# Attention products moved from VectorE to GpSimd, the token statistics of the next tile moved behind those of the last, and a finer final conversion

## The chip, the cores and the metric

One Trainium2 chip, all 8 cores. Each core takes 2,048 of the 16,384 tokens and runs the same program; no core talks to another. The metric is the device time of the slowest core in microseconds (us).

## The reference

```python
def _layernorm(x, axis=-1, eps=1e-5):
    m = jnp.mean(x, axis=axis, keepdims=True)
    v = jnp.var(x, axis=axis, keepdims=True)
    return (x - m) / jnp.sqrt(v + eps)

# attention: the 16 heads of ONE token attend to each other, D_K = 64
qkv = (jnp.einsum('bsd,de->bse', x, W_qkv) + b_qkv).reshape(B, S, 16, 3 * 64)
q, k, v = (qkv[..., :64], qkv[..., 64:128], qkv[..., 128:])
scores = jnp.einsum('bshd,bsgd->bshg', q, k) / np.sqrt(64)
attn = jax.nn.softmax(scores, axis=-1)
context = jnp.einsum('bshg,bsgd->bshd', attn, v).reshape(B, S, 1024)
attn_out = jnp.einsum('bsd,de->bse', context, W_out) + b_out

# ffn: 8 experts, all of them for every token, summed
h = jax.nn.silu(x @ wg) * (x @ wu);  acc = acc + h @ wd     # 1024 -> 4096 -> 1024

x = x + _layernorm(attn_ref(_layernorm(x)))
x = x + _layernorm(ffn_ref(_layernorm(x)))
```

The input is 16,384 tokens of 1,024 float32 numbers.

## The kernel before

The program is written as one list of instructions for each engine, with semaphores placed by hand. Each engine works through its list strictly in order, so the order of the calls in the source is the order on each engine. It has three stages.

Stage A is the attention, over 16 tiles of 128 tokens, tokens on the partitions. A tile t goes through: S1 (layer norm of the input, `ln_stats` at L141 and the write of `ln1` at L230), S2 (8 transposes on TensorE at L206 and their copy out of PSUM by VectorE at L209), S3 (54 matmuls for q, k and v, L253 and L257, each of 6 groups copied to `qkv` by ScalarE at L262), S4 (the attention proper, on VectorE), S5 (transposes of `ctxt`, the output projection at L359), S6 (layer norm of the projection and its addition to `xf`, L163 to L379) and S7 (the second layer norm, transposes into `ln2T`; for every fourth tile SyncE spills `xf` to HBM and loads new tokens).

S4 first copies v into `vtc` in another order (L272). Then, for 4 groups of 4 heads, it multiplies q by k into a 4,096-wide bf16 product `prod` (L283), halves it by three additions (L287) and sums the last 8 columns into `scores` (L292). `prod` has two slots, so group n may be written once group n-2 has been summed. A softmax follows (L297 to L311), its Exp on ScalarE (L305), and then 4 groups of the product with v (L325, L329, L337). In the kernel before all of this but the Exp is VectorE's.

The layer norms pass through ScalarE: L154 and L156 (Ln and Exp on a column) sit in ScalarE's list behind whatever stands before them. The loop at L406 sets that list:

```python
    S1(0)
    for t_i in range(nt_lim):
        S2(t_i)
        S3(t_i)
        if t_i + 1 < nt_lim:
            S1(t_i + 1)
        if t_i >= 1:
            S6(t_i - 1)
            S7(t_i - 1)
        S4(t_i)
        S5(t_i)
```

Stage B is the feed-forward part. 64 blocks of weights (8 experts by 8 slices of 512) are loaded by GpSimd's queue into double buffers; for each block and each of 4 groups of 512 tokens (jj), TensorE makes gate and up products (L498, L503), ScalarE the silu (L509), VectorE the product `hbuf` (L513), and TensorE the down product (L529), which VectorE adds to `acc` in SBUF (L539). The down product of a group runs one group behind.

Stage C waits until all of `acc` is written, converts it to bf16 on ScalarE in 8 rows of 2,048 (L583), and then takes 16 tiles: 8 transposes (L600), copy, layer norm on VectorE (L604 to L625), the addition of the spilled `xf` (`xrel`, loaded per tile at L593), and the store (L634).

Of the kernel before, what the change touches and what calls it, by code (L numbers as in the profile page):

```python
# [26 lines left out]

def build(mode='full', nt_lim=NT):
    nc = bass.Bass("TRN2", target_bir_lowering=False)
    x_d = nc.dram_tensor("x", [T, D], F32, kind="ExternalInput").ap()  # L30
    wqkv_d = nc.dram_tensor("wqkv", [D, H3], F32, kind="ExternalInput").ap()
    bqkv_d = nc.dram_tensor("bqkv", [H3], F32, kind="ExternalInput").ap()
    wout_d = nc.dram_tensor("wout", [D, D], F32, kind="ExternalInput").ap()
# [49 lines left out]
    XLa = Ch("XLa"); XLb = Ch("XLb")  # L83
    STa = Ch("STa"); STb = Ch("STb")
    STD = Ch("STD")
    XC = Ch("XC")
    SP = Ch("SP")
    STp = [None, None]
    WI = Ch("WI")
# [31 lines left out]
    ps_mm = Pa("ps_mm", [128, 2, 512], F32)  # L121
    ps_att = Pa("ps_att", [128, 2, 2, 512], F32)

    x_r = x_d.rearrange("(j i p) d -> p j i d", p=128, i=4)
    xsp_r = xsp_d.rearrange("(j i p) d -> p j i d", p=128, i=4)
    op('y', lambda e: e.dma_start(xf[:, 0], x_r[:, 0]), XLa, 16)
    op('y', lambda e: e.dma_start(xf[:, 1], x_r[:, 1]), XLb, 16)
    op('g', lambda g: g.dma_start(wqkv_sb[:], wqkv_d.rearrange("(k p) e -> p k e", p=128)), WI, 16)
# [139 lines left out]
    def S4(t_i):  # L268
        p2 = t_i % 2
        QE.wt('v', tok_qkv_ev_last[t_i])  # L270
        qb = 3072 * p2
        op('v', lambda v, qb=qb: v.tensor_copy(  # L272
            vtc[:].rearrange("p (d g) -> p d g", g=16),
            bass.AP(qh, qb + 128, [[2 * H3, 128], [1, 64], [192, 16]])), VV)
        for grp in range(4):
            h0 = grp * 4
            gg = n_hg[0]; n_hg[0] += 1
            sl = gg % 2
            if gg - 2 in tok_prod:
                VV.wt('v', tok_prod[gg - 2])  # L280
            qap = bass.AP(qh, qb + 192 * h0, [[2 * H3, 128], [192, 4], [0, 16], [1, 64]])
            kap = bass.AP(qh, qb + 64, [[2 * H3, 128], [0, 4], [192, 16], [1, 64]])
            op('v', lambda v, sl=sl, qap=qap, kap=kap: v.tensor_tensor(  # L283
                prod[:, sl].rearrange("p (h g d) -> p h g d", h=4, g=16), qap, kap, ALU.mult), VV)
            VV.wt('v')
            for half in (32, 16, 8):
                op('v', lambda v, sl=sl, half=half: v.tensor_add(  # L287
                    bass.AP(prod, sl * 4096, [[8192, 128], [1024, 4], [64, 16], [1, half]]),
                    bass.AP(prod, sl * 4096, [[8192, 128], [1024, 4], [64, 16], [1, half]]),
                    bass.AP(prod, sl * 4096 + half, [[8192, 128], [1024, 4], [64, 16], [1, half]])), VV)  # L290
                VV.wt('v')
# [22 lines left out]
        VV.wt('v')  # L314
        if t_i >= 2:
            TB.wt('v', tok_ctx_tr[t_i - 2])
        for grp in range(4):
            h0 = grp * 4
            gg = n_hg[0]; n_hg[0] += 1
            sl = gg % 2  # L320
            if gg - 2 in tok_prod:
                VV.wt('v', tok_prod[gg - 2])
            pap = bass.AP(ph, 16 * h0, [[256, 128], [16, 4], [0, 64], [1, 16]])
            vap = bass.AP(vtc, 0, [[1024, 128], [0, 4], [16, 64], [1, 16]])
            op('v', lambda v, sl=sl, pap=pap, vap=vap: v.tensor_tensor(  # L325
                prod[:, sl].rearrange("p (h d g) -> p h d g", h=4, d=64), pap, vap, ALU.mult), VV)
# [349 lines left out]
```

How the kernel before makes its waits and increments, by code:

```python
        def wt(self, k, tok=None):  # L71
            t_ = self.v if tok is None else tok
            em(k, lambda e, h=self.h, t=t_: e.wait_ge(h, t))
# [1 line left out]
    def op(k, fn, ch=None, n=1):  # L75
        if ch is not None:
            ch.v += n
            em(k, lambda e, fn=fn, h=ch.h, n=n: fn(e).then_inc(h, n))
            return ch.v
        em(k, fn)
        return None
```

## Time and profile before

| what | us |
|---|---|
| median of 3 runs | 7795.84 |
| lowest and highest run | 7694.49, 7986.77 |
| the profiled execution | 7065.31 |
| its span (slowest core, core 7) | 7063.7 |
| spans of the 8 cores | 7056.4 to 7063.7 |
| mean granted TensorE clock, every core | 0.905 |

The profiled execution is one run with its own record of every instruction. Its span runs from the first to the last instruction of the slowest core; 1.6 us of its time lie around the span. The eight cores agree, so one core may be read for all. The profiled execution is shorter than the lowest of the runs. Busy time of an engine is the sum of its instructions' durations; idle time is shown with the engine that released the wait.

### The profile page before, as it was taken

What the parts mean: (1) busy time and instruction counts of PE and PEld (TensorE: products, weight loads), DVE (VectorE), ACT (ScalarE), POOL (GpSimd) and SP (SyncE); (2) the same over time, 40 slices, a digit from 0 to 9 for tenths busy, and PEclk for the clock granted to TensorE, in tenths of its full rate; (3) what the DMA queues carried; (4) which work ended last, traced back from release to release, by engine and by line L of the source; (5) the groups of instructions that cost most, each with busy time, mean ns of one, the idle gap of its engine ahead of it and who ended that gap; (6) DMA issues with size and microseconds to landing.
All of it is one profiled execution on the core that took longest, in us unless ns stands there. A gap on an engine that the chain in (4) does not pass through costs nothing.

```text
span 7063.7 us, 71318 instructions; the slowest of 8 cores (7056.4 to 7063.7 us)
## 1 busy us (share of the span) xinstructions
PE 5675.5 (80%) x26240; PEld 2558.7 (36%) x26240; DVE 3241.3 (46%) x4484; ACT 745.9 (11%) x1291; POOL 165.0 (2%) x202
## 2 busy tenths in 40 slices
PE   2212222219999999999999999999999999999991
PEld 0000000104444444444444444444444444444441
DVE  3767666653343443434343434343434343443436
ACT  0000000001111111111111111111111111111111
POOL 0000000000000000000000000000000000000000
PEclk8556666659999999999999999999999999999995
DMA  3000000012223222222232222223322222232212
GB/s 71 0 24 0 24 0 12 0 25 41 36 39 46 42 36 36 36 36 36 42 47 38 36 36 36 36 36 45 46 36 36 36 37 36 39 46 42 36 19 95
DMA packets 178221, 247.85 MB, mean 35 GB/s; under 512 B 3808, under 2 KB 134880, under 8 KB 177888
## 3 DMA queue, kind: packets, MB, share of 16 engines
q0 software_dynamic: 169056, 209.74, 19.9%
q1 hardware_dynamic: 8832, 33.56, 1.4%
q8 instruction: 223, 3.65, 0.2%
q14 instruction: 110, 0.90, 0.0%
HBM read 436.22 MB, written 16.78 MB: 64 GB/s over the span
## 4 chain that ended last, share of the span: by engine, by line
PE 80%; DVE 14%; issue 3%; ACT 1%; another core or an unknown queue 1%; DMA 0%; DVEq 0%; ACTq 0%; POOL 0%; POOLq 0%
PE ps_g L498 25%; PE ps_u L503 25%; PE ps_d L529 25%; PE ps_mm L257 3%; DVE prod L329 2%; DVE prod L287 2%; DVE prod L325 2%; DVE prod L283 2%; PE ps_att L359 1%; PE ps_tr L206 1%; DMA wd_b<-wd 0%; PE ps_mm L253 0%; DVEq L73 0%; DVE tmpl L375 0%
## 5 line engine op out<-in xcount | busy, mean ns | idle before, releaser
L513 DVE TENSOR_TENSOR hbuf<-silb,ps_u 128x512 bf16<-128x512 bf16 x1024 | 704.7, 688 | 2886.4 <-PE ps_u L503 2845.8
L498 PE MATMUL ps_g<-ln2T,wg_b 128*128 128x512 bf16 x8192 | 1936.9, 379 | 35.8 <-DMA wd_b<-wd 35.8
L503 PE MATMUL ps_u<-ln2T,wu_b 128*128 128x512 bf16 x8192 | 1935.3, 379 | 0.0
L529 PE MATMUL ps_d<-hbuf,wd_b 128*128 128x512 bf16 x8192 | 1809.7, 379 | 0.0
L539 DVE TENSOR_TENSOR acc<-ps_d,acc 128x512 f32<-128x512 f32 x2016 | 1392.9, 692 | 330.6 <-PE ps_d L529 303.5
L498 PEld LDWEIGHTS ps_g<-ln2T,wg_b 128*128 128x128 bf16 x8192 | 801.7, 98 | 1003.4 <-issue 37.7
L503 PEld LDWEIGHTS ps_u<-ln2T,wu_b 128*128 128x128 bf16 x8192 | 801.8, 98 | 966.7 <-issue 0.7
L529 PEld LDWEIGHTS ps_d<-hbuf,wd_b 128*128 128x128 bf16 x8192 | 801.6, 98 | 966.5
L509 ACT ACTIVATE silb<-ps_g 128x512 bf16<-128x512 f32 x1024 | 611.3, 597 | 4675.2 <-PE ps_g L498 4675.2
L206 PE MATMUL ps_tr<-ident,ctxt 128*128 128x128 bf16 x128 | 16.2, 305 | 824.4 <-DVE ctxt L337 824.4
L206 PEld LDWEIGHTS ps_tr<-ident,ctxt 128*128 128x128 bf16 x128 | 12.3, 136 | 828.4 <-issue 828.4
L206 PE MATMUL ps_tr<-ident,ln2tok 128*128 128x128 bf16 x128 | 16.2, 305 | 274.9 <-DVE ln2tok L391 274.9
L470 POOL DMA_DIRECT2D wg_b<-wg x64 | 56.9, 890 | 6590.5 <-PE ps_d L529 5030.4
L257 PE MATMUL ps_mm<-wqkv_sb,ln1T 128*128 128x512 bf16 x768 | 184.2, 383 | 0.0
L329 DVE TENSOR_TENSOR prod<-prod 128x2048 bf16<-128x2048 bf16 (+2 forms) x192 | 162.3, 845 | 20.7 <-DVE prod L329 0.9
L287 DVE TENSOR_TENSOR prod<-prod 128x2048 bf16<-128x2048 bf16 (+2 forms) x192 | 149.9, 781 | 20.4 <-DVE prod L283 0.5
L325 DVE TENSOR_TENSOR prod<-probsn,vtc 128x4096 bf16<-128x4096 bf16 x64 | 146.3, 2286 | 3.7 <-DVE probsn L311 3.7
L283 DVE TENSOR_TENSOR prod<-qkv 128x4096 bf16<-128x4096 bf16 x64 | 146.1, 2282 | 0.0
L262 ACT ACTIVATE qkv<-ps_mm 128x512 bf16<-128x512 f32 x96 | 57.3, 597 | 695.0 <-PE ps_mm L257 695.0
L206 PEld LDWEIGHTS ps_tr<-ident,ln2tok 128*128 128x128 bf16 x128 | 12.4, 136 | 282.3 <-issue 282.3
L600 PE MATMUL ps_c<-ident,acc_bf 128*128 128x128 bf16 x128 | 16.0, 306 | 114.9 <-DVE acctok L604 99.2
L257 PEld LDWEIGHTS ps_mm<-wqkv_sb,ln1T 128*128 128x128 bf16 x768 | 67.6, 98 | 91.4 <-issue 24.2
(80 smaller groups left out, 974.2 us busy)
## 6 DMA issues: line engine op xcount, KB each, us to landing
wg_b<-wg POOLq DMA_DIRECT2D x64, 1024.0 KB, 12.4
wu_b<-wu POOLq DMA_DIRECT2D x64, 1024.0 KB, 18.2
wd_b<-wd POOLq DMA_DIRECT2D x64, 1024.0 KB, 22.2
xf<-x SPq DMA_DIRECT2D x4, 2048.0 KB, 13.9
xspill<-xf SPq DMA_DIRECT2D x4, 2048.0 KB, 6.9
xrel<-xspill SPq DMA_DIRECT2D x16, 512.0 KB, 3.9
out<-outb SPq DMA_DIRECT2D x16, 512.0 KB, 2.9
wqkv_sb<-wqkv POOLq DMA_DIRECT2D x1, 6144.0 KB, 53.5
```

Of the source, the lines that this page charges most:

```text
L206: tr_tok = op('t', lambda t, k=k, s_=s_: t.transpose(ps_tr[:, s_, k], src_fn(k), ident[:]), TB if k == 7 else None)
L257: mt = op('t', lambda t, n=n, b=b, k=k, p2=p2: t.matmul(ps_mm[:, b], ln1T[:, p2, k], wqkv_sb[:, k, n * 512:(n + 1) * 512], start=False, st ...
L283: op('v', lambda v, sl=sl, qap=qap, kap=kap: v.tensor_tensor(prod[:, sl].rearrange("p (h g d) -> p h g d", h=4, g=16), qap, kap, ALU.mult) ...
L287: op('v', lambda v, sl=sl, half=half: v.tensor_add(bass.AP(prod, sl * 4096, [[8192, 128], [1024, 4], [64, 16], [1, half]]), bass.AP(prod, ...
L325: op('v', lambda v, sl=sl, pap=pap, vap=vap: v.tensor_tensor(prod[:, sl].rearrange("p (h d g) -> p h d g", h=4, d=64), pap, vap, ALU.mult) ...
L329: op('v', lambda v, sl=sl, half=half: v.tensor_add(bass.AP(prod, sl * 4096, [[8192, 128], [1024, 4], [16, 64], [1, half]]), bass.AP(prod, ...
L498: gt = op('t', lambda t, par=par, kh=kh, kd=kd, bk=bk, toks=toks: t.matmul(ps_g[:, bk], wg_b[:, par, kd, kh * 128:(kh + 1) * 128], ln2T[:, ...
L503: ut = op('t', lambda t, par=par, kh=kh, kd=kd, bk=bk, toks=toks: t.matmul(ps_u[:, bk], wu_b[:, par, kd, kh * 128:(kh + 1) * 128], ln2T[:, ...
L509: silu_tok[c] = op('s', lambda s, bk=bk, c=c: s.activation(silb[:, c % 2], ps_g[:, bk], AF.Silu), SIL)
L513: mul_tok[c] = op('v', lambda v, kh=kh, bk=bk, c=c, q=q: v.tensor_tensor(hbuf[:, q % 2, kh], silb[:, c % 2], ps_u[:, bk], ALU.mult), MUL)
L529: dt_ = op('t', lambda t, par=par, m=m, mi=mi, kh=kh, q=q: t.matmul(ps_d[:, mi], wd_b[:, par, kh, m * 128:(m + 1) * 128], hbuf[:, q % 2, k ...
L539: tok = op('v', lambda v, m=m, mi=mi, toks=toks: v.tensor_add(acc[:, m, toks], ps_d[:, mi], acc[:, m, toks]), ACC)
```

## The change

Four things are edited. First, in S4 the copy into `vtc` and the four multiplications of q by k go from VectorE's list to GpSimd's, with a new semaphore GP; GpSimd waits for the last copy of q, k and v (QE), for the end of the previous tile's S4, and for `prod`'s slot. The three additions and the sum stay on VectorE. Second, S1 of the next tile is called after S6 and S7 of the last one. Third, in stage C the conversion is cut into 16 pieces of 8 by 128 columns, and each group of four pieces waits only for its own token group's last addition; `acc_bf` gets memory of its own from stage B's start, the transposes wait for their own piece, and `xrel` is loaded in 4 transfers of 2 MB with two slots, not 16 of 512 KB. Fourth, x, out and the spill lie in HBM as partition by tile by column.

```diff
-    x_d = nc.dram_tensor("x", [T, D], F32, kind="ExternalInput").ap()
+    x_d = nc.dram_tensor("x", [128, NT, D], F32, kind="ExternalInput").ap()
...
-    out_d = nc.dram_tensor("out", [T, D], F32, kind="ExternalOutput").ap()
-    xsp_d = nc.dram_tensor("xspill", [T, D], F32, kind="Internal").ap()
+    out_d = nc.dram_tensor("out", [128, NT, D], F32, kind="ExternalOutput").ap()
+    xsp_d = nc.dram_tensor("xspill", [128, NT, D], F32, kind="Internal").ap()
...
         QE.wt('v', tok_qkv_ev_last[t_i])
+        QE.wt('g', tok_qkv_ev_last[t_i])
+        if t_i >= 1:
+            VV.wt('g', tok_hm_done[t_i - 1])
         qb = 3072 * p2
-        op('v', lambda v, qb=qb: v.tensor_copy(
+        op('g', lambda g, qb=qb: g.tensor_copy(
             vtc[:].rearrange("p (d g) -> p d g", g=16),
-            bass.AP(qh, qb + 128, [[2 * H3, 128], [1, 64], [192, 16]])), VV)
+            bass.AP(qh, qb + 128, [[2 * H3, 128], [1, 64], [192, 16]])), GP)
...
             if gg - 2 in tok_prod:
-                VV.wt('v', tok_prod[gg - 2])
+                VV.wt('g', tok_prod[gg - 2])
...
-            op('v', lambda v, sl=sl, qap=qap, kap=kap: v.tensor_tensor(
-                prod[:, sl].rearrange("p (h g d) -> p h g d", h=4, g=16), qap, kap, ALU.mult), VV)
-            VV.wt('v')
+            op('g', lambda g, sl=sl, qap=qap, kap=kap: g.tensor_tensor(
+                prod[:, sl].rearrange("p (h g d) -> p h g d", h=4, g=16), qap, kap, ALU.mult), GP)
+            GP.wt('v')
...
-        if t_i + 1 < nt_lim:
-            S1(t_i + 1)
         if t_i >= 1:
             S6(t_i - 1)
             S7(t_i - 1)
+        if t_i + 1 < nt_lim:
+            S1(t_i + 1)
         S4(t_i)
...
-    ACC.wt('s', B_acc_done)
-    conv_tok = None
-    for mrow in range(8):
-        conv_tok = op('s', lambda s, mrow=mrow: s.activation(acc_bf[:, mrow], acc[:, mrow], AF.Copy),
-                      CS if mrow == 7 else None)
...
+    conv_tok = {}
+    for t_c in range(NT):
+        g_jj = t_c // 4
+        if t_c % 4 == 0:
+            ACC.wt('s', accw_tok[((NE * NG - 1) * NJ + g_jj, 1, 3)])
+        conv_tok[t_c] = op('s', lambda s, t_c=t_c: s.activation(
+            acc_bf[:, :, t_c * 128:(t_c + 1) * 128],
+            acc[:, :, t_c * 128:(t_c + 1) * 128], AF.Copy), CS)
...
+    for g_jj in range(2):
+        op('y', lambda e, g_jj=g_jj: e.dma_start(
+            xrel[:, g_jj % 2], xsp_r[:, g_jj]), XCa if g_jj % 2 == 0 else XCb, 16)
...
-        op('y', lambda e, t_i=t_i, p2=p2: e.dma_start(xrel[:, p2], xsp_t[:, t_i]), XC, 16)
         if t_i == 0:
-            CS.wt('t', conv_tok)
+            ACC.wt('t', B_acc_done)
+        CS.wt('t', conv_tok[t_i])
```

How the lists move. VectorE in stage A, around the head of a tile, before: `ln1T` is the copy that releases the q, k and v matmuls, `scr`/`stats` from `xf` are S1, `stats` from `ps_att` is S6.

```order
L209 COPY ln1T<-ps_tr 128x1024
L143 TENSOR_TENSOR scr<-xf 128x1024
L144 TENSOR_REDUCE stats<-xf 128x1
...
L158 TENSOR_SCALAR stats<-stats 128x1
L230 TENSOR_SCALAR ln<-xf,stats 128x1024
L163 TENSOR_REDUCE stats<-ps_att 128x1
L167 TENSOR_REDUCE stats<-scr 128x1
```

The same place of VectorE's list after the change (its line numbers are one higher there).

```order
L210 COPY ln1T<-ps_tr 128x1024
L164 TENSOR_REDUCE stats<-ps_att 128x1
L168 TENSOR_REDUCE stats<-scr 128x1
L169 TENSOR_SCALAR stats<-stats 128x1
L171 TENSOR_SCALAR stats<-stats 128x1
L172 TENSOR_TENSOR stats<-stats 128x1
L174 TENSOR_TENSOR stats<-stats 128x1
```

One reduction now stands between the copy and the next instruction that needs ScalarE (L168, which reads ScalarE's square); before, seven instructions of S1 stood between the copy and L158.

VectorE at the head of S4, before: the last copy of S7, then the copy of v, a product, its halvings and its sum.

```order
L209 COPY ln2T<-ps_tr 128x8x128
L272 COPY vtc<-qkv 128x1024
L283 TENSOR_TENSOR prod<-qkv 128x4096
L287 TENSOR_TENSOR prod<-prod 128x64x32
L287 TENSOR_TENSOR prod<-prod 128x64x16
L287 TENSOR_TENSOR prod<-prod 128x64x8
L292 TENSOR_REDUCE scores<-prod 128x64
```

The same place after: the end of S1, then the halvings at once, and GpSimd's own list for the same tile in the second piece.

```order
L159 TENSOR_SCALAR stats<-stats 128x1
L231 TENSOR_SCALAR ln<-xf,stats 128x1024
L291 TENSOR_TENSOR prod<-prod 128x64x32
L291 TENSOR_TENSOR prod<-prod 128x64x16
L291 TENSOR_TENSOR prod<-prod 128x64x8
L296 TENSOR_REDUCE scores<-prod 128x64
```

```order
L133 MEMSET ident 128x128
L135 AFFINE_SELECT ident<-ident 128x128
L276 COPY vtc<-qkv 128x1024
L287 TENSOR_TENSOR prod<-qkv 128x4096 x4
```

VectorE's five instructions of S4's head have become three kinds, and GpSimd, whose list held nothing between L135 and the weight loads, has a copy and four products per tile.

## Rows read from the trace of the kernel before

**Rows 1.** The page: busy time, share of the span and instructions by engine.
```profile
PE 5675.5 (80%) x26240; PEld 2558.7 (36%) x26240; DVE 3241.3 (46%) x4484; ACT 745.9 (11%) x1291; POOL 165.0 (2%) x202
```

**Rows 2.** Stretches of stages A, B and C; columns named in the first line.
```profile
core 7: us, PE busy (x) PEld busy (x) DVE busy (x) ACT busy (x) POOL busy (x), PEclk, DMA share, GB/s
0.00:1565.00 1565.00, 353.29 (x1536) 141.18 (x1536) 1011.91 (x1236) 108.09 (x225) 3.68 (x10) 0.63 0.06 15
1565.00:6906.00 5341.00, 5306.22 (x24576) 2405.08 (x24576) 2118.76 (x3071) 612.61 (x1025) 161.33 (x192) 1.00 0.26 39
6906.00:7064.00 158.00, 16.03 (x128) 12.46 (x128) 110.67 (x177) 25.20 (x41) 0.00 (x0) 0.53 0.30 106
```

**Rows 3.** Timeline of a tile: start, duration, engine, line; idle before in brackets.
```profile
529.59 0.69 DVE L209 COPY ln1T<-ps_tr 128x1024 bf16<-128x1024 bf16 x1 [8.36 <-PE ps_tr L206]
...
534.35 0.16 DVE L152 TENSOR_TENSOR stats<-stats 128x1 f32<-128x1 f32 x1
...
543.58 0.60 ACT L262 ACTIVATE qkv<-ps_mm 128x512 bf16<-128x512 f32 x1 [1.55 <-PE ps_mm L257]
...
544.86 0.21 DVE L158 TENSOR_SCALAR stats<-stats 128x1 f32<-128x1 f32 x1 [10.34 <-ACT stats L156]
...
547.28 1.02 ACT L165 ACTIVATE scr<-ps_att 128x1024 f32<-128x1024 f32 x1 [2.54 <-DVE stats L163]
...
550.12 0.16 DVE L173 TENSOR_TENSOR stats<-stats 128x1 f32<-128x1 f32 x1
...
554.26 1.23 DVE L143 TENSOR_TENSOR scr<-xf 128x1024 f32<-128x1024 f32 x1
...
559.86 0.81 DVE L391 TENSOR_SCALAR ln2tok<-xf,stats 128x1024 bf16<-128x1024 f32 x1 [0.18 <-DVE stats L158]
...
562.66 1.02 DVE L272 COPY vtc<-qkv 128x1024 bf16<-128x1024 bf16 x1
...
565.98 2.55 DVE L287 TENSOR_TENSOR prod<-prod 128x2048 bf16<-128x2048 bf16 x3
568.63 0.69 DVE L292 TENSOR_REDUCE scores<-prod 128x64 f32<-128x512 bf16 x1
...
585.91 0.69 DVE L292 TENSOR_REDUCE scores<-prod 128x64 f32<-128x512 bf16 x1
...
622.72 0.69 DVE L209 COPY ln1T<-ps_tr 128x1024 bf16<-128x1024 bf16 x1 [7.27 <-PE ps_tr L206]
```

**Rows 4.** Groups of instructions on GpSimd: count, busy us and mean ns, idle.
```profile
L134 POOL TENSOR_SCALAR_AFFINE_SELECT ident<-ident 128x128 bf16<-128x128 bf16 x1 | 0.3, 287 | 0.2 <-POOL ident L132 0.2
L132 POOL MEMSET ident<- 128x128 bf16 x1 | 0.2, 248 | 0.0
L29 POOL MEMSET const-bfloat16-1.0<- 128x1 bf16 x1 | 0.1, 101 | 0.0
```

**Rows 5.** Groups on VectorE, stage A until 1200 us, shapes kept apart.
```profile
L287 DVE TENSOR_TENSOR prod<-prod 128x2048 bf16<-128x2048 bf16 x48 | 58.8, 1225 | 5.4 <-DVE prod L283 0.5
L230 DVE TENSOR_SCALAR ln<-xf,stats 128x1024 bf16<-128x1024 f32 x14 | 11.4, 813 | 2.7 <-DVE stats L158 2.5
```

**Rows 6.** Timeline of the end of stage B and the head of stage C.
```profile
6906.09 0.69 DVE L539 TENSOR_TENSOR acc<-ps_d,acc 128x512 f32<-128x512 f32 x1 [0.17 <-PE ps_d L529]
6906.17 0.33 SPq L593 DMA_DIRECT2D xrel<-xspill  x1
6906.87 14.50 ACT L583 ACTIVATE acc_bf<-acc 128x2048 bf16<-128x2048 f32 x8 [15.68 <-DVE acc L539]
6921.52 2.97 PE L600 MATMUL ps_c<-ident,acc_bf 128*128 128x128 bf16 x24 [15.54 <-ACT acc_bf L583]
6931.23 1.23 DVE L632 TENSOR_TENSOR outb<-xrel,tmpc 128x1024 f32<-128x1024 f32 x1 [0.17 <-DVE tmpc L625]
```

**Rows 7.** The page's DMA issues: KB each, median us from issue to landing.
```profile
xf<-x SPq DMA_DIRECT2D x4, 2048.0 KB, 13.9
```

**Rows 8.** The additions of stage C: duration min/median/max, first and last start.
```profile
L632 DVE TENSOR_TENSOR outb<-xrel,tmpc x16: 1224/1226/1227, 6931.2 to 7059.4; 128x1024 f32<-128x1024 f32 x16
```

More of the change, by code:

```diff
@@ L85, in build @@
     STD = Ch("STD")
-    XC = Ch("XC")
+    XCa = Ch("XCa"); XCb = Ch("XCb")
     SP = Ch("SP")
@@ L98, in build @@
     CS = Ch("CS")
+    GP = Ch("GP")
     TB = Ch("TB")
@@ L122, in build @@
     ps_att = Pa("ps_att", [128, 2, 2, 512], F32)
-    x_r = x_d.rearrange("(j i p) d -> p j i d", p=128, i=4)
-    xsp_r = xsp_d.rearrange("(j i p) d -> p j i d", p=128, i=4)
+    x_r = x_d.rearrange("p (j i) d -> p j i d", i=4)
+    xsp_r = xsp_d.rearrange("p (j i) d -> p j i d", i=4)
     op('y', lambda e: e.dma_start(xf[:, 0], x_r[:, 0]), XLa, 16)
@@ L316, in S4 @@
             TB.wt('v', tok_ctx_tr[t_i - 2])
+        GP.wt('v')
         for grp in range(4):
@@ L437, in build @@
     acc = acc_ctx.enter_context(nc.sbuf_tensor("acc", [128, 8, T], F32))
+    acc_bf = acc_ctx.enter_context(nc.sbuf_tensor("acc_bf", [128, 8, T], BF16))
     bctx = ExitStack()
@@ L571, in build @@
     Pc = lambda n, sh, dt: c2.enter_context(nc.psum_tensor(n, sh, dt))
-    acc_bf = Sc("acc_bf", [128, 8, T], BF16)
     acctok = Sc("acctok", [128, 2, D], BF16)
-    xrel = Sc("xrel", [128, 2, D], F32)
+    xrel = Sc("xrel", [128, 2, 4, D], F32)
     tmpc = Sc("tmpc", [128, 2, D], F32)
@@ L578, in build @@
     ps_c = Pc("ps_c", [128, 2, 8, 128], BF16)
-    ACC.wt('s', B_acc_done)
-    conv_tok = None
-    for mrow in range(8):
-        conv_tok = op('s', lambda s, mrow=mrow: s.activation(acc_bf[:, mrow], acc[:, mrow], AF.Copy),
-                      CS if mrow == 7 else None)
-    xsp_t = xsp_d.rearrange("(ti p) d -> p ti d", p=128)
-    out_t = out_d.rearrange("(ti p) d -> p ti d", p=128)
+    conv_tok = {}
[6 more added lines that the diff above has]
+            acc[:, :, t_c * 128:(t_c + 1) * 128], AF.Copy), CS)
+    xsp_t = xsp_d
+    out_t = out_d
     tok_c_ev = {}
@@ L590, in build @@
     MMD.wt('y'); WLa.wt('y'); WLb.wt('y')
+    for g_jj in range(2):
+        op('y', lambda e, g_jj=g_jj: e.dma_start(
+            xrel[:, g_jj % 2], xsp_r[:, g_jj]), XCa if g_jj % 2 == 0 else XCb, 16)
+    tok_c_add = {}
     for t_i in range(NT):
         p2 = t_i % 2
-        op('y', lambda e, t_i=t_i, p2=p2: e.dma_start(xrel[:, p2], xsp_t[:, t_i]), XC, 16)
         if t_i == 0:
-            CS.wt('t', conv_tok)
+            ACC.wt('t', B_acc_done)
+        CS.wt('t', conv_tok[t_i])
         if t_i >= 2:
@@ L627, in build @@
         VV.wt('v')
-        XC.wt('v', 16 * (t_i + 1))
+        XCj = XCa if (t_i // 4) % 2 == 0 else XCb
+        XCj.wt('v', 16 * ((t_i // 4) // 2 + 1))
         if t_i >= 2:
@@ L631, in build @@
             SPT.wt('v', tok_c_st[t_i - 2])
-        st_tok = op('v', lambda v, p2=p2: v.tensor_add(outb[:, p2], xrel[:, p2], tmpc[:, p2]), VV)
+        st_tok = op('v', lambda v, t_i=t_i: v.tensor_add(
+            outb[:, t_i % 2], xrel[:, (t_i // 4) % 2, t_i % 4], tmpc[:, t_i % 2]), VV)
+        tok_c_add[t_i] = st_tok
+        if t_i % 4 == 3 and t_i // 4 + 2 < NJ:
+            g_jj = t_i // 4 + 2
+            VV.wt('y', st_tok)
+            op('y', lambda e, g_jj=g_jj: e.dma_start(
+                xrel[:, g_jj % 2], xsp_r[:, g_jj]), XCa if g_jj % 2 == 0 else XCb, 16)
         VV.wt('y', st_tok)
@@ L657 @@
     nc = _cache['nc']
-    x = np.ascontiguousarray(np.asarray(L0_attn_x, dtype=np.float32).reshape(NCORE * T, D))
+    x = np.asarray(L0_attn_x, dtype=np.float32).reshape(NCORE * T, D)
     wqkv = np.ascontiguousarray(np.asarray(L0_attn_W_qkv, dtype=np.float32))
@@ L668 @@
         in_maps.append({
-            "x": np.ascontiguousarray(x[c * T:(c + 1) * T]),
+            "x": np.ascontiguousarray(
+                x[c * T:(c + 1) * T].reshape(NT, 128, D).swapaxes(0, 1)),
             "wqkv": wqkv, "bqkv": bqkv, "wout": wout, "bout": bout,
@@ L673 @@
     res = run_bass_kernel_spmd(nc, in_maps, core_ids=list(range(NCORE)))
-    out = np.concatenate([r["out"] for r in res.results], axis=0)
+    out = np.concatenate(
+        [r["out"].swapaxes(0, 1).reshape(T, D) for r in res.results], axis=0)
     return out.reshape(1, NCORE * T, D)
```

## The prediction, made before the changed kernel ran

> **What bounds the kernel now.** I read the busy times first, then three stretches cut at the stages, then the timeline of one tile in stage A, then the hand-over from stage B to C. The reader is to see that the busy shares mislead: TensorE is busy for 80% of the span [rows 1], but that is stage B, which the change leaves alone (5306 of 5341 us busy [rows 2]). The change works in stages A and C. In stage A, 1565 us long, VectorE is busy 1012 us and GpSimd 4 us [rows 2], so giving GpSimd work looks free. The timeline says where VectorE's time goes in a tile. From one copy of `ln1T` to the next is 622.72 - 529.59 = 93.1 us [rows 3]. VectorE's idle stretches in it are 7.3 us for TensorE at the tile's head and 10.3 us for ScalarE, whose column functions stand behind the last copy of q, k and v, which ends at 543.58 + 0.60 = 544.2 [rows 3]. From there until S5 VectorE goes on almost without a gap and is the chain that sets the tile. So an edit pays by what it takes off VectorE after 544.2, and GpSimd cannot begin before 544.2 either, since it needs the same q, k and v.
>
> **The move of S1.** Before, S1's statistics run in the shade of the matmuls, up to 534.35 + 0.16 [rows 3]. Now only S6's first reduction is there, and ScalarE's square, which began at 547.28, may begin at 544.2, so what follows it comes 3.1 us earlier: S7's copy ends at 562.66 - 3.1 = 559.6. Then S1 runs in full; as S7, which has the same instructions, it takes 559.86 + 0.81 - 554.26 = 6.4 us. VectorE reaches S4 at 566.0 instead of 562.7 [rows 3]. The move costs 3.3 us, and buys GpSimd time for its first two products.
>
> **The products on GpSimd.** VectorE gives up the copy and four products. With products on GpSimd of length p the remaining work per group is 2.55 + 0.69 us, 3.25 with the overlap of rows [rows 3]. No row shows a two-input operation on GpSimd. The nearest ones are the affine select, (287 - 101) / 127 = 1.46 ns a column with one input and one output, and the memset, (248 - 101) / 127 = 1.16 ns with no input [rows 4]. The product reads two streams and writes one. If a stream costs half the affine select's 1.46, it is 1.5 times that: 2.2 ns x 4096 + 0.1 = 9.1 us. The ends are 4.8 us (as a memset) and 12.1 us (each input like a whole select); 6.1 us is the select itself. I take 9.1, between the select and twice it, and 2 us for the strided copy of 1024 columns. GPSIMD Engine Reference of the Trainium skill, section on performance versus the Vector engine, gives 4497 ns for a 2048-column float32 add, which would make an estimate of 9.0 us here; no run before shows it.
>
> **Do the two engines run side by side?** This decides more than p. The rows give both ends only indirectly: no computing GpSimd instruction lies beside a computing VectorE one. The bound from below is that neither delays the other. The bound from above is that a VectorE instruction with two SBUF inputs starts only when GpSimd's instruction has ended. What speaks for the upper end in rows: a 1024-column `tensor_scalar` on one SBUF input takes 813 ns while the same width with two float32 inputs takes 1.23 us [rows 3, 5]; VectorE has a second way into SBUF, which the two-input instructions need all the time, and GpSimd must enter somewhere. I take the upper end. The Trainium skill, SBUF — State Buffer, section on the two sides of SBUF, states it outright: VectorE and GpSimd share one read and write port pair as an exclusive lock, held for the whole instruction, and a VectorE operation with two SBUF inputs blocks against a GpSimd one that reads SBUF. No run before shows this; by its opposite the sum would be the first rival's.
>
> **The walk of a tile, taking turns.** GpSimd: copy 544.3 to 546.3, products 0 and 1 to about 564.7 (2 x 9.1 and two gaps). VectorE's small two-input statistics of S6 come due at 550.12 - 3.1 = 547.0 and wait; L173 can start at 564.7 instead. From L173 to the end of S7 is 562.66 - 550.12 = 12.5 us, then S1's 6.4: S4 starts at 583.6. In that time GpSimd idles, because product 2 waits for the sum of group 0. Then: group 0's halvings and sum 3.25; group 1's first halving (1.2 us, [rows 5]) gets in before product 2; product 2 takes 9.1 with VectorE's second halving waiting behind it; the rest of group 1 takes 2.1; the same again with group 2's first halving (1.2), product 3 (9.1) and the rest (2.1); group 3 takes 3.25. In sum 583.6 + 3.25 + 1.2 + 9.1 + 2.1 + 1.2 + 9.1 + 2.1 + 3.25 = 614.9. Before, the last sum ended at 585.91 + 0.69 = 586.6 [rows 3]. So a tile becomes 28.3 us longer; as p enters four times, that is 4p - 8.1. Behind it softmax, the products with v and S5 are unchanged, and GpSimd, which waits for the end of S4, does nothing beside them. Times 16 tiles: +453 us. (The first tile has no S6 and S7 to hide anything and comes to about the same.)
>
> **Stage C.** The conversion takes 14.5 us with everybody waiting [rows 6]. In pieces, twelve of sixteen run while TensorE finishes its last down products, and the transposes can start at 6907 instead of 6921.5: -14.6 us. The conversion of a late piece (1.0 us, as the 1024-column square in [rows 3]) keeps ahead of VectorE's tile of (7059.4 - 6931.2) / 15 = 8.5 us [rows 8]. But the first `xrel` transfer is now 2 MB with a second behind it. Issued at 6906.2, at the 13.9 us of an equal load [rows 7] it lands at 6920.1; the first addition came 6931.23 - 6921.52 = 9.7 us after the transposes and would be due at 6916.6. So up to 3.5 us come back (nothing if the load is quicker, about 10 more if the two transfers interleave), and I put stage C at -12 us. The new layout of x, out and spill changes only how long the pieces are; the 4 MB at the start lie under the load of the weights of q, k and v, the others under whole tiles: 0, and at most a few us either way.
>
> **Sum.** Against the profiled execution: 7065 + 453 - 12 = 7506 us. The median of the runs is 731 us above that execution. Stage B is the part that follows TensorE's clock, at 1.00 there in the profile, and I expect the surplus in it; both my terms are VectorE's and GpSimd's times, which that clock does not touch. I carry the difference over whole: 7796 + 441 = 8237 us, 5.7% longer.
>
> **The rivals.**
> - Side by side, p = 9.1. S4 starts at 566.0, group 0 is summed at 569.3, products 2 and 3 follow back to back to 587.6, the last group ends at 590.9: 4.3 us a tile longer. 16 x 4.3 + 12 for the first tile (nothing covers its first two products) - 12 = +69 us, 7865, within 2%. For it: the trace has nothing that forbids it. Against: the second way into SBUF above.
> - Not slower at all: side by side and a cheap product, p = 4.8, the memset's price. Then product 3 ends at 579.0, the tile at 582.3, 4.3 us earlier; 16 x -4.3 - 12 = -81 us, 7715. It decides from p below about 7 us, where 2p - 13.9 turns negative. The floor is 16 x -7.4 - 12 = -130 us (VectorE's own 4 x 3.25 from 566.0), 1.7%, so faster by more than 2% needs a further gain that I cannot name.
> - Taking turns with p = 6.1: 4p - 8.1 = 16.3, +249 us, 8045, 3.2% slower. With p = 12.1: 40.3, +633 us, 8429.
> - The edit of stage C fails of its aim (both transfers land late): 10 us at most, inside every case.
>
> **How the numbers follow.** Taking turns near p = 9: 0.50; taking turns, cheaper or dearer: 0.18; side by side near 9: 0.22; side by side and cheap, not slower: 0.10. 2%, 156 us, is about what a measurement of this kernel can tell from no change. Slower by over 2% are the turn-taking cases: 0.68; within 2%: 0.29; faster by over 2%: 0.03. The range reaches from just under the first rival, 7840, to just under the dear end of turn-taking, 8420; outside it lie the cheap side-by-side cases and the dearest products.
>
> **What would show it.** In the changed profile: GpSimd's product rows should read near 9.1 us each, 64 of them, 580 us and more in all; VectorE's halvings should have a mean far above 1.2, 0.7 and 0.4 us, or idle time behind GpSimd; the `ln1T` copies should be 121 us apart; PE's first L600 should start within 1 us of the last L539. If the halvings keep their durations and the tile is 97 us, the turn-taking is wrong. If product rows read 5 us or 13 us, p is. If stage B's length differs at the same clock, the whole frame is wrong.

## The result and the profile after

| what | before | after |
|---|---|---|
| median of the runs, us | 7343.35 (10 runs) | 7428.11 (8 runs) |
| shortest run, us | 7064.51 | 7413.05 |
| span of a core at full clock in stage B, us | 7063.7 | 7408.9 |

The ratio of after to before is 1.0502, 95% interval 1.0476 to 1.0528: the changed kernel is slower, by 5%. Many runs of either kernel, and four cores of the profiled run after, show a lower TensorE clock in stage B (core 0 after: 6007 us at a granted clock of 0.88, where core 5 has 5341 at 1.00); the ratio leaves those runs out (the medians do not), and the rows below are of core 5, which is not touched.

The time came in stage A. This is the same view as [rows 2], of core 5 after, cut where its stages end.

```profile
0.00:1925.00 1925.00, 360.02 (x1536) 142.16 (x1536) 1321.41 (x1156) 108.13 (x225) 564.28 (x90) 0.61 0.05 12
1925.00:7266.00 5341.00, 5307.10 (x24576) 2405.25 (x24576) 2118.95 (x3071) 624.07 (x1037) 161.35 (x192) 1.00 0.27 39
7266.00:7409.00 143.00, 14.87 (x129) 11.44 (x128) 110.68 (x177) 14.59 (x37) 0.00 (x0) 0.52 0.32 118
```

Stage A is 360 us longer, stage B has its 5341 us again, stage C is 15 us shorter. And VectorE, from whose list the copy of v and the 64 products were taken (16 and 146 us), is busy 310 us more in stage A, not 162 less. A busy sum that grows when work is taken away is the sign to look at single rows. The timeline of one tile after answers to [rows 3]; it starts at 638.52 where that one starts at 529.59.

```profile
638.52 0.69 DVE L210 COPY ln1T<-ps_tr 128x1024 bf16<-128x1024 bf16 x1 [7.90 <-PE ps_tr L207]
...
652.52 0.60 ACT L263 ACTIVATE qkv<-ps_mm 128x512 bf16<-128x512 f32 x1 [1.55 <-PE ps_mm L258]
653.01 1.02 ACT L166 ACTIVATE scr<-ps_att 128x1024 f32<-128x1024 f32 x1
653.30 1.93 POOL L276 COPY vtc<-qkv 128x1024 bf16<-128x1024 bf16 x1 [56.71 <-ACT qkv L263]
...
655.18 15.71 POOL L287 TENSOR_TENSOR prod<-qkv 128x4096 bf16<-128x4096 bf16 x2
655.27 0.14 DVE L169 TENSOR_SCALAR stats<-stats 128x1 f32<-128x1 f32 x1
655.52 0.15 DVE L171 TENSOR_SCALAR stats<-stats 128x1 f32<-128x1 f32 x1
655.59 7.50 DVE L172 TENSOR_TENSOR stats<-stats 128x1 f32<-128x1 f32 x1
663.19 7.73 DVE L174 TENSOR_TENSOR stats<-stats 128x1 f32<-128x1 f32 x1
671.01 0.29 ACT L176 ACTIVATE stats<-stats,consts 128x1 f32<-128x1 f32 x1 [16.98 <-DVE stats L174]
...
689.61 2.54 DVE L291 TENSOR_TENSOR prod<-prod 128x2048 bf16<-128x2048 bf16 x3
692.26 0.69 DVE L296 TENSOR_REDUCE scores<-prod 128x64 f32<-128x512 bf16 x1
692.86 10.03 DVE L291 TENSOR_TENSOR prod<-prod 128x2048 bf16<-128x2048 bf16 x3
693.09 8.72 POOL L287 TENSOR_TENSOR prod<-qkv 128x4096 bf16<-128x4096 bf16 x1 [22.19 <-DVE scores L296]
702.99 0.69 DVE L296 TENSOR_REDUCE scores<-prod 128x64 f32<-128x512 bf16 x1
703.60 10.03 DVE L291 TENSOR_TENSOR prod<-prod 128x2048 bf16<-128x2048 bf16 x3
703.82 8.72 POOL L287 TENSOR_TENSOR prod<-qkv 128x4096 bf16<-128x4096 bf16 x1 [2.01 <-DVE scores L296]
713.73 0.69 DVE L296 TENSOR_REDUCE scores<-prod 128x64 f32<-128x512 bf16 x1
...
716.97 0.69 DVE L296 TENSOR_REDUCE scores<-prod 128x64 f32<-128x512 bf16 x1
```

The multiplication of one column by one column (L172), 0.15 us before, is shown as 7.50 us long, and the subtraction behind it as 7.73. The first ends with GpSimd's first product (663.09 against 655.18 + 15.71 / 2 = 663.04), the second with both (670.92 against 670.89). The one-column `tensor_scalar` instructions L169 and L171 take 0.14 and 0.15 us although GpSimd is at work. The three halvings are 10.03 us long whenever a product runs and 2.54 when none does. The wait is not shown as idle time; it is inside the duration of the waiting instruction.

Grouped by shape, the same on the whole of VectorE (count, busy us, mean ns, idle before), to be read against [rows 5]:

```profile
L291 DVE TENSOR_TENSOR prod<-prod 128x1024 bf16<-128x1024 bf16 x64 | 283.5, 4430 | 7.0 <-DVE prod L291 0.5
...
L174 DVE TENSOR_TENSOR stats<-stats 128x1 f32<-128x1 f32 x16 | 115.7, 7234 | 2.0 <-DVE stats L172 0.5
L172 DVE TENSOR_TENSOR stats<-stats 128x1 f32<-128x1 f32 x16 | 112.5, 7031 | 0.0
L291 DVE TENSOR_TENSOR prod<-prod 128x2048 bf16<-128x2048 bf16 x64 | 85.4, 1335 | 7.8 <-POOL prod L287 7.8
```

The first halving (2048 columns) gets in ahead of the product and keeps nearly its 1225 ns [rows 5] (mean 1335); the second (1024 columns) is the one that waits, with a mean of 4430 ns where it had 692. GpSimd's own groups, which answer to [rows 4]:

```profile
L287 POOL TENSOR_TENSOR prod<-qkv 128x4096 bf16<-128x4096 bf16 x64 | 530.6, 8301 | 364.1 <-DVE scores L296 364.1
...
L276 POOL COPY vtc<-qkv 128x1024 bf16<-128x1024 bf16 x16 | 30.7, 1918 | 936.7 <-ACT qkv L263 936.7
```

8301 ns is a mean of two kinds: products 0 and 1, 15.71 / 2 = 7.86 us, and products 2 and 3, 8.72, which are issued while VectorE's first halving runs. So the wait goes both ways. Stage C's start, against [rows 6]:

```profile
7266.25 0.79 SPq L600 DMA_DIRECT2D xrel<-xspill  x2
...
7267.11 1.05 PE L612 MATMUL ps_c<-ident,acc_bf 128*128 128x128 bf16 x16 [1.05 <-DVE acc L545]
7267.83 0.69 DVE L616 COPY acctok<-ps_c 128x1024 bf16<-128x1024 bf16 x1 [0.96 <-PE ps_c L612]
...
7276.42 1.23 DVE L645 TENSOR_TENSOR outb<-xrel,tmpc 128x1024 f32<-128x1024 f32 x1 [0.17 <-DVE tmpc L637]
```

The transposes start 0.9 us after the SyncE issue; before, they started at 6921.52 after an issue at 6906.17, 15.4 us later [rows 6]. The first addition has only 0.17 us of idle before it, as in [rows 6]: the 2 MB transfer was there in time.

### The profile page after: what moved, and what is told of

It is laid out like the page before. It is cut to its first block, busy times and chain, and to the rows that moved or that the text cites. A ratio compares the mean times of both kernels' runs of the same rounds, so it can differ in the third digit from the quotient of the medians.

```text
span 8077.6 us, 71382 instructions; the slowest of 8 cores (7408.9 to 8077.6 us)
## 1 busy us (share of the span) xinstructions
PE 6352.2 (79%) x26240; PEld 2715.5 (34%) x26240; DVE 3549.9 (44%) x4404; ACT 747.0 (9%) x1299; POOL 725.7 (9%) x282
## 4 chain that ended last, share of the span: by engine, by line
PE 78%; DVE 17%; issue 2%; another core or an unknown queue 1%; ACT 1%; DMA 0%; DVEq 0%; POOL 0%; ACTq 0%; POOLq 0%
PE ps_d L535 25%; PE ps_g L504 25%; PE ps_u L509 25%; DVE prod L291 5%; PE ps_mm L258 2%; DVE prod L334 2%; DVE prod L330 2%; DVE stats L174 1%; DVE stats L172 1%; PE ps_att L364 1%; PE ps_tr L207 1%; DVE stats L147 0%; DVE scr L144 0%; DVE stats L145 0%
## 5 line engine op out<-in xcount | busy, mean ns | idle before, releaser
L504 PE MATMUL ps_g<-ln2T,wg_b 128*128 128x512 bf16 x8192 | 2164.9, 412 | 33.4 <-DMA wd_b<-wd 33.4
L509 PE MATMUL ps_u<-ln2T,wu_b 128*128 128x512 bf16 x8192 | 2163.9, 412 | 0.0
L535 PE MATMUL ps_d<-hbuf,wd_b 128*128 128x512 bf16 x8192 | 2035.8, 413 | 0.0
L504 PEld LDWEIGHTS ps_g<-ln2T,wg_b 128*128 128x128 bf16 x8192 | 853.7, 104 | 1171.0 <-issue 765.3
L535 PEld LDWEIGHTS ps_d<-hbuf,wd_b 128*128 128x128 bf16 x8192 | 854.1, 104 | 1138.6 <-issue 738.8
L509 PEld LDWEIGHTS ps_u<-ln2T,wu_b 128*128 128x128 bf16 x8192 | 853.4, 104 | 1137.0 <-issue 730.3
L287 POOL TENSOR_TENSOR prod<-qkv 128x4096 bf16<-128x4096 bf16 x64 | 530.6, 8301 | 363.9 <-DVE scores L296 363.9
L291 DVE TENSOR_TENSOR prod<-prod 128x2048 bf16<-128x2048 bf16 (+2 forms) x192 | 396.1, 2063 | 21.9 <-POOL prod L287 7.8
L334 DVE TENSOR_TENSOR prod<-prod 128x2048 bf16<-128x2048 bf16 (+2 forms) x192 | 162.2, 845 | 20.3 <-DVE prod L334 0.5
L174 DVE TENSOR_TENSOR stats<-stats 128x1 f32<-128x1 f32 x16 | 115.7, 7234 | 2.0 <-DVE stats L172 0.5
L276 POOL COPY vtc<-qkv 128x1024 bf16<-128x1024 bf16 x16 | 30.7, 1919 | 939.7 <-ACT qkv L263 939.7
```

The source lines that it names most:

```text
L174: op('v', lambda v: v.tensor_sub(st_[:, 2:3], st_[:, 1:2], st_[:, 2:3]), VV)
L287: op('g', lambda g, sl=sl, qap=qap, kap=kap: g.tensor_tensor(prod[:, sl].rearrange("p (h g d) -> p h g d", h=4, g=16), qap, kap, ALU.mult) ...
L291: op('v', lambda v, sl=sl, half=half: v.tensor_add(bass.AP(prod, sl * 4096, [[8192, 128], [1024, 4], [64, 16], [1, half]]), bass.AP(prod, ...
L334: op('v', lambda v, sl=sl, half=half: v.tensor_add(bass.AP(prod, sl * 4096, [[8192, 128], [1024, 4], [16, 64], [1, half]]), bass.AP(prod, ...
L504: gt = op('t', lambda t, par=par, kh=kh, kd=kd, bk=bk, toks=toks: t.matmul(ps_g[:, bk], wg_b[:, par, kd, kh * 128:(kh + 1) * 128], ln2T[:, ...
L509: ut = op('t', lambda t, par=par, kh=kh, kd=kd, bk=bk, toks=toks: t.matmul(ps_u[:, bk], wu_b[:, par, kd, kh * 128:(kh + 1) * 128], ln2T[:, ...
```

## The experiments

The tile distance below is (last minus first start of the `ln1T` copies) / 15; it is (1459.4 - 78.8) / 15 = 92.0 us before and (1799.0 - 76.3) / 15 = 114.8 us after. Times are set against the kernel before in the same batch, whose shortest runs were 7063.6 to 7065.4 us. Where there is no interval, I give the shortest run and the tile distance.

**1. The products back on VectorE.** The changed kernel without its first edit.

```diff
-        op('g', lambda g, qb=qb: g.tensor_copy(
+        op('v', lambda g, qb=qb: g.tensor_copy(
...
-            op('g', lambda g, sl=sl, qap=qap, kap=kap: g.tensor_tensor(
+            op('v', lambda g, sl=sl, qap=qap, kap=kap: g.tensor_tensor(
```

> The changed kernel with the copy of v and the four products back on VectorE; the late S1, stage C and the layout stay. Taking turns (my theory): the loss goes, what is left is the late S1, 3.3 us for each of 15 tiles, less 15 us of stage C: 7065 + 50 - 15 = 7100 us, ratio to before 1.005, tile distance 96.4 us. Rival (the order of S1, not GpSimd, makes the loss): near the changed kernel, 1.04 or more.

Three of four runs lie at 7090.4 to 7092.7 us, 1.0035 times before; the tile distance is (1500.7 - 77.1) / 15 = 94.9 us. The move to GpSimd makes the loss; the late S1, with the products on VectorE, costs 2.9 us a tile (3.3 expected).

**2. S1 early again, the products on GpSimd.**

```diff
+        if t_i + 1 < nt_lim:
+            S1(t_i + 1)
         if t_i >= 1:
             S6(t_i - 1)
             S7(t_i - 1)
-        if t_i + 1 < nt_lim:
-            S1(t_i + 1)
```

> The changed kernel with S1 again ahead of S6 and S7; the products stay on GpSimd. Taking turns: GpSimd's first two products hold VectorE wherever its work stands, so the late S1 buys nothing; S6 is freed at the same time after the head of the tile and S4 starts 6.4 us earlier, 15 x 6.4 = 96 us less than the changed kernel: 7317 us, ratio 1.036. Rival (the late S1 covers GpSimd's products, no turns): 3 us a tile more than the changed kernel, ratio 1.055 or so.

There is no ratio here. The shortest run is 7373.3 us; cores 0 to 3 of the profiled run have spans of 7310.5 to 7317.0 us, 7317 expected. The tile distance is (1708.2 - 78.1) / 15 = 108.7 us, 6.1 less than after. The late S1 did not cover the products: without it they still hold S6 until they end, and the tile is shorter. The rival falls. Rows of core 0, the head of a tile:

```profile
630.61 1.89 POOL L276 COPY vtc<-qkv 128x1024 bf16<-128x1024 bf16 x1 [56.02 <-ACT qkv L263]
...
631.48 1.58 DVE L231 TENSOR_SCALAR ln<-xf,stats 128x1024 bf16<-128x1024 f32 x1 [0.18 <-DVE stats L159]
632.47 16.16 POOL L287 TENSOR_TENSOR prod<-qkv 128x4096 bf16<-128x4096 bf16 x2
...
636.87 3.94 DVE L172 TENSOR_TENSOR stats<-stats 128x1 f32<-128x1 f32 x1
640.92 7.73 DVE L174 TENSOR_TENSOR stats<-stats 128x1 f32<-128x1 f32 x1
```

S6's first two-input instruction (L172) comes later here, in the middle of the first product, and is held 3.94 us instead of 7.50; L174 again ends with the second product. A third kind shows too: L231, a `tensor_scalar` on 1024 columns of SBUF, 0.81 us before [rows 5], takes 1.58 us beside GpSimd's copy and ends 0.6 us after it, and the two products behind it are 16.16 us long, not 15.71. It has one tensor input, but it is quicker than the two-input instructions of the same width (1.23 us), so it too uses more than one way into SBUF (a reading of the rows; not tried apart).

**3. Stage C and the layout alone**, on the kernel before; run twice.

> The kernel before with only the fine conversion of stage C, the 2 MB loads of xrel and the layout. Theory: 15 us less, ratio 0.998, stages A and B as before. Rival (the layout or the shared memory of acc_bf costs or gains somewhere): any other ratio than 0.9965 to 0.9995.

> e3_stage_c once more, for an interval: 7050 us, ratio 0.998; stage A ends and stage B lasts as before, stage C is 15 us shorter. Rival (the layout costs or gains in stage A): the last copy of ln2T more than 3 us away from where it is in the kernel before.

The first batch's shortest run was 7049.9 us. The second gave ratio 0.9983, interval 0.9954 to 1.0013, and five runs at 7047.9 to 7049.3 us against a shortest 7063.6 before: 15 us less, though the interval alone does not tell it from nothing. The last `ln2T` copy has to be set core against core, for in the kernel before it starts anywhere from 1559.6 to 1564.1, by the core. In cores 4 to 7 of the profiled run it starts 1.5 us later, 4.4, 2.3 and 1.5 us earlier than in the same core before. One core is outside the 3 us that I had set; the tile distance, 91.9 to 92.0 us in all four, is that of before (91.9 to 92.0). So no cost of the layout shows in stage A.

**4. A memset in place of the products** (the multiplication of q by k is left out): GpSimd writes SBUF and reads nothing.

```diff
-            op('g', lambda g, sl=sl, qap=qap, kap=kap: g.tensor_tensor(
-                prod[:, sl].rearrange("p (h g d) -> p h g d", h=4, g=16), qap, kap, ALU.mult), GP)
+            op('g', lambda g, sl=sl: g.memset(prod[:, sl], 0.0), GP)
```

> The changed kernel with a memset of the same 4096 columns on GpSimd in place of each product, so the product of q and k is left out. GpSimd then writes SBUF but reads nothing. Theory (the turns are about reading SBUF): VectorE's halvings are back at 1.22, 0.69 and 0.42 us and the two statistics L172 and L174 at 0.15 us though GpSimd is busy beside them; S4's first half takes 4 x 3.25 us, the tile is 7.4 us shorter than before, 7065 - 118 - 15 = 6932 us, ratio 0.981. Rival (any GpSimd instruction holds VectorE): 4.8 us each by the ident memset, 4p - 8.1 = 11 us a tile longer, 7228 us, ratio 1.023.

Ratio 0.9829 (0.9806 to 0.9853), tile distance 85.9 us. Rows of its timeline:

```profile
603.88 6.96 POOL L287 MEMSET prod<- 128x4096 bf16 x2
604.29 0.15 DVE L172 TENSOR_TENSOR stats<-stats 128x1 f32<-128x1 f32 x1
604.55 0.16 DVE L174 TENSOR_TENSOR stats<-stats 128x1 f32<-128x1 f32 x1
...
626.65 2.54 DVE L290 TENSOR_TENSOR prod<-prod 128x2048 bf16<-128x2048 bf16 x3
626.86 6.97 POOL L287 MEMSET prod<- 128x4096 bf16 x2 [16.01 <-DVE scores L295]
```

Beside GpSimd's memsets the two statistics take 0.15 and 0.16 us, and three halvings their 2.54. The same engines, buffers and semaphores; the reading is gone, and with it the turns. The multiplication is gone too and the instruction is shorter, which the next experiment tells apart. A memset takes 6.96 / 2 = 3.5 us, not the 4.8 that I had from the short one of [rows 4].

**5. A copy in place of the products** (q is left out): one read stream.

```diff
-                prod[:, sl].rearrange("p (h g d) -> p h g d", h=4, g=16), qap, kap, ALU.mult), GP)
+                prod[:, sl].rearrange("p (h g d) -> p h g d", h=4, g=16), kap), GP)
```

> The changed kernel with a copy of k (4096 columns, one input) on GpSimd in place of each product, so the multiplication by q is left out. Theory: one read stream on GpSimd is enough to hold VectorE's two-input instructions for the whole instruction; at 6.1 us each by the affine select's price a tile is 16 us longer than before, 7065 + 261 - 15 = 7311 us, ratio 1.035; L172 and L174 as long as a copy. Rival (only GpSimd's second input collides): the halvings at their own times, ratio 0.99.

Ratio 1.0101 (1.0081 to 1.0121), 7139.3 us, tile distance (1544.7 - 77.1) / 15 = 97.8 us.

```profile
571.53 7.15 POOL L287 COPY prod<-qkv 128x4096 bf16<-128x4096 bf16 x2
571.63 0.14 DVE L169 TENSOR_SCALAR stats<-stats 128x1 f32<-128x1 f32 x1
571.88 0.15 DVE L171 TENSOR_SCALAR stats<-stats 128x1 f32<-128x1 f32 x1
571.95 3.19 DVE L172 TENSOR_TENSOR stats<-stats 128x1 f32<-128x1 f32 x1
575.25 3.44 DVE L174 TENSOR_TENSOR stats<-stats 128x1 f32<-128x1 f32 x1
```

The copy is as long as the memset, 7.15 / 2 = 3.6 us, and multiplies nothing either, but it reads, and it holds L172 and L174. Experiments 4 and 5 together settle it. The mechanism was as expected, the price was not: 3.6 us are far under my 6.1, and the hold shrinks with it. It tests the prediction's formula at a second point: 4 x 3.6 - 8.1 = 6.3 us a tile, measured 97.8 - 92.0 = 5.8.

**6. Two of four groups on GpSimd.**

```diff
+            pe = 'g' if grp < 2 else 'v'
+            PCH = GP if grp < 2 else VV
```

> The changed kernel with only groups 0 and 1 of the products (and the copy of v) on GpSimd, groups 2 and 3 on VectorE. Taking turns: S4's first half is 2 x 3.25 + 2 x 5.65 = 17.8 us instead of 28.1, 10.3 us a tile less than the changed kernel, 7249 us, ratio 1.026; the two holds of S6 stay at 7.5 us each. Rival (products 2 and 3 were hidden and only the first two cost): no change, ratio 1.05.

The shortest run is 7250.8 us, 1.0264 times the shortest before (1.026 expected), tile distance (1650.0 - 77.9) / 15 = 104.8 us. L172 and L174 stand at 7.49 and 7.73 us as in the changed kernel. So to have products 2 and 3 on GpSimd costs 10.0 us a tile (10.3 expected).

**7. The two statistics with one tensor input.**

```diff
-        op('v', lambda v: v.tensor_mul(st_[:, 2:3], st_[:, 0:1], st_[:, 0:1]), VV)
+        op('v', lambda v: v.tensor_scalar(st_[:, 2:3], st_[:, 0:1], st_[:, 0:1], None, ALU.mult), VV)
...
-        op('v', lambda v: v.tensor_sub(st_[:, 2:3], st_[:, 1:2], st_[:, 2:3]), VV)
+        op('v', lambda v: v.tensor_scalar(st_[:, 2:3], st_[:, 1:2], st_[:, 2:3], None, ALU.subtract), VV)
```

> The changed kernel with the square of the mean and the variance in the layer norms of stage A written as operations of one tensor and a column as scalar, the same numbers. Theory (two SBUF tensor inputs is what makes an instruction wait): L172 and L174 run in 0.15 us beside GpSimd; VectorE goes on to the addition L384, the next instruction with two inputs, and is held there until a product ends; 2.6 us a tile less, 7372 us, ratio 1.0435. Rival (any VectorE instruction on SBUF is held): the same columns are held for 7.5 us each, ratio 1.050.

Ratio 1.0452 (1.0384 to 1.0520), shortest run 7362.0 us, tile distance 111.8 us, 3.0 less than after. The interval is too wide to part 1.0435 from 1.050; the rows and the tile distance do:

```profile
644.39 16.70 POOL L287 TENSOR_TENSOR prod<-qkv 128x4096 bf16<-128x4096 bf16 x2
...
644.79 0.20 DVE L172 TENSOR_SCALAR stats<-stats 128x1 f32<-128x1 f32 x1
...
645.10 0.21 DVE L174 TENSOR_SCALAR stats<-stats 128x1 f32<-128x1 f32 x1
...
647.97 5.39 DVE L384 TENSOR_TENSOR xf<-xf,tmpl 128x1024 f32<-128x1024 f32 x1
653.46 8.71 DVE L144 TENSOR_TENSOR scr<-xf 128x1024 f32<-128x1024 f32 x1
```

The same values, computed without a second tensor input, take 0.20 and 0.21 us beside a product. The wait goes to the next two-input instructions: L384 gets in between the products (which are 16.70 us long together, 1.0 more than the 15.71 after), and L144 waits out the second one.

**8. The idle time at the head of the tile.** Products on VectorE, stage C as changed, and S6 called ahead of S3.

```diff
         S2(t_i)
+        if t_i >= 1:
+            S6(t_i - 1)
         S3(t_i)
         if t_i >= 1:
-            S6(t_i - 1)
             S7(t_i - 1)
```

> All products on VectorE, stage C as changed, and S6 of the last tile called ahead of S3, so that its square, Ln and Exp stand ahead of the copies of q, k and v in ScalarE's list; then S3, S7, S1. Theory (VectorE's wait for ScalarE at the tile's head is the loss to be had): S6 runs in the shade of the matmuls, S7's statistics too, S4 starts 7 us earlier than in the kernel before: 7065 - 15 x 7 - 15 = 6945 us, ratio 0.983. Rival (delaying the copies of q, k and v delays TensorE and S4 by as much): ratio 0.998 or above.

> e8_early_s6 once more, for an interval: 6932 us was its shortest run, ratio 0.981 expected; a ratio above 0.99 would say that the first look was a matter of the runs.

The first batch's shortest run was 6932.1 us. The second gave ratio 0.9805 (0.9770 to 0.9839), shortest run 6931.7 us; tile distance (1352.4 - 77.9) / 15 = 85.0 us, 7.0 less than before. It beats both kernels. About 15 us of the gain are stage C's; against experiment 3, which has the same stage C, the move of S6 is 7047.9 - 6931.7 = 116 us, 1.6%. VectorE's waits in stage A, in us, times and longest, before:

```profile
DVE stats L158 <- ACT stats L156: 157.9, 29, 10.6
```

and in this version:

```profile
DVE stats L159 <- ACT stats L157: 59.7, 30, 3.4
```

**9. One more thing off VectorE**, the square in S1's layer norm, to ScalarE, on top of 8.

```diff
...
+            VV.wt('s')
+            op('s', lambda s: s.activation(scr[:, par], src_fn(), AF.Square), SS)
...
```

> e8_early_s6 with the square of S1's layer norm (tiles 2 and up) on ScalarE, where it finds the engine idle behind S7's Exp and runs beside VectorE's ln2tok write and wait for the transposes. Theory (whatever leaves VectorE after the copies of q, k and v is gained whole, if the engine that takes it shares nothing with VectorE): 1.22 us a tile, 14 x 1.2 = 17 us less than e8: 6915 us, ratio 0.979. Rival (a second handover between engines eats it): no change against e8.

Ratio 0.9844 (0.9782 to 0.9907), shortest run 6925.2 us; the eight spans are 6916.7 to 6923.7 us against 6926.4 to 6931.0 in experiment 8, 8 us less, not 17. The intervals overlap; the spans do not. In S1 itself the 1.2 us are gained, but VectorE's wait for the transposes at the tile's head grows, from 106.3 to 116.5 us over stage A. TensorE's output projection in stage A (experiment 8, core 3, then 9, core 7):

```profile
L360 PE MATMUL ps_att<-wout_sb,ctxT 128*128 128x512 bf16 x256 | 86.9, 501 | 0.0
```

```profile
L367 PE MATMUL ps_att<-wout_sb,ctxT 128*128 128x512 bf16 x256 | 95.7, 541 | 0.0
```

It takes 8.8 us more over the stage (4 to 12 us, core against the same core), and VectorE waits for what stands behind it. In one tile, the granted clock of that stretch was 0.57, against 0.65 in experiment 8: less of it at 2.4 GHz and more at 1.2. Neither theory had this. What sets the moment of the clock's rise there was not tried, so that this is the cause of the missing gain is argued, not shown.

## Why the prediction was right or wrong

**The cause: right, and shown.** The prediction chose that a two-input VectorE instruction starts only when GpSimd's has ended. Experiments 4, 5 and 7 tell this from the rivals: take away GpSimd's reading, or VectorE's second input, and the wait of that instruction is gone while both engines stay busy. The Trainium skill, SBUF — State Buffer, section on the two sides of SBUF, had the rule; every run here agrees, also in that only a GpSimd instruction that reads SBUF holds a two-input one (L172: 0.15 us beside a memset, 3.19 beside a copy of the same length). The two side-by-side rivals fall with the row of L172, 7.50 us.

**The walk of the tile: right, with one size off.** Every step is found: the one-column statistics held for two products, the first halving ahead of product 2 and the second behind it, GpSimd idle for 22 us in between. The mis-sized term is p: 9.1 us taken, 7.9 measured. I had priced a stream at half the affine select's cost, the same for reads and writes. Measured, 4096 columns cost 3.5 us written only, 3.6 read and written, 7.9 with two reads and a multiplication: the first read is all but free beside the write. Whether the second read or the multiplication doubles the price, no run tells. The Trainium skill's figure for a float32 add (GPSIMD Engine Reference, section on performance versus the Vector engine), from which the prediction had an estimate of 9.0 us, would have been too high too for this bf16 product. With 7.9 the formula gives 4 x 7.9 - 8.1 = 23.5 us; the tile distance grew by 114.8 - 92.0 = 22.8, where the prediction had 28.3, and stage A by 360 us, where it had 453.

**The move of S1: right.** 3.3 us said, 2.9 measured in experiment 1. That it "buys GpSimd time for its first two products" was wrong by the prediction's own walk, in which VectorE waits while they run; experiment 2 shows that with the products on GpSimd the late S1 buys nothing and costs 6.1 us a tile.

**Stage C: nearly right.** -12 us said, -15 measured in the profile and in experiment 3; the transposes come 0.25 us after the last addition ends, within the 1 us said. The term that was off is the 3.5 us for a late `xrel`: the transfer was there by 10.2 us after its issue, not at 13.9, and nothing came back. The rival that the edit fails of its aim falls.

**Stage B: right.** 5341 us at a clock of 1.00 in both.

**The sum: the step that failed is the last.** Against the profiled execution the prediction had 7506 us, +441; the shortest run is 7413.05, +349 on 7064.5, and 16 x 4 x 1.2 = 77 us of the difference are p. But the forecast was then moved to 8237 us, and the range to 7840 to 8420, because the whole 731 us between the median of three runs and the profiled execution was carried over as a term of the sum. It is no fixed term. In the ten runs of before that the result rests on, the median is 7343.35 - 7064.51 = 279 us above the shortest run, with three runs at 7064.5 to 7065.2; in the eight runs after, it is 7428.11 - 7413.05 = 15 us above it. That the surplus lies in stage B was right as far as core 0 after shows it. The measured 7428 lies under the range for that reason: 731 us lower, the same range would be 7109 to 7689 and hold it. In ratio, 5.7% were forecast and 5.0% came, which is nearer than the working was: part of it is that the 441 us were divided by 7796, and on 7065 they are 6.2%. One slip had no effect: the floor of the second rival is 7.6 us a tile by its own terms (566.0 + 4 x 3.25 = 579.0, against 586.6), not 7.4.

## What to carry to other kernels

An idle engine is not free capacity. Before work that reads SBUF is moved to GpSimd beside VectorE, count the two-input VectorE instructions that will run beside it. Each of them, one column wide or a thousand, waits for the end of the GpSimd instruction that is running, and the profile shows it as a long instruction, not as idle time. Here the gain lay in the order of one in-order list (experiment 8: 1.6% by moving a call), which showed as a 10 us wait in every tile. When a few runs scatter by more than the change under study, forecast from the profiled execution, and give the change as a ratio.

## What the runs showed of the hardware that was not expected

- The wait is counted as busy time: VectorE's busy sum in stage A rose from 1012 to 1321 us while 162 us of work were taken from it.
- A one-column instruction is held like a wide one: 0.15 us became 7.50 (L172).
- GpSimd's queue of two products does not shut VectorE out for both: a waiting VectorE instruction gets in between them (L172 after the first, L174 after the second; experiment 7: L384 ends 5.39 us after its start, then L144 waits 8.71).
- The wait goes both ways: GpSimd's products 2 and 3, issued while VectorE's first halving runs, are 8.72 us long, and products 0 and 1 are 7.86.
- On GpSimd, 4096 bf16 columns: memset 3.5 us, copy 3.6, two-input product 7.9; a copy of 1024 columns with a stride 1.9 us (L276).
- A fast one-input `tensor_scalar` (0.81 us) was held by GpSimd's copy (1.58 us, experiment 2), a one-column one was not (0.14 us beside a product).
- With 1.2 us a tile taken off VectorE (experiment 9), TensorE's projection in stage A took 4 to 12 us more in all, at a lower granted clock (0.57 against 0.65 in one tile). Why was not tried.
